# Four residual blocks on one Trainium2 core: the quantized FFN's zero points added by accumulating transfers, and one more down column taken by ScalarE

## The chip, the cores and the metric

One Trainium2 chip (trn2), one core of it. The metric is the device time of one execution in microseconds (us), lower is better. The engines are named PE (TensorE), DVE (VectorE), ACT (ScalarE), POOL (GpSimd) and SP (SyncE, which here only issues transfers).

## The reference

`x` is 8 x 128 x 512 in float32, 1024 tokens of width 512. Four residual blocks follow each other, each behind a layer norm:

```
x = x + xattn0(ln(x), ctx)
x = x + ffn0(ln(x))                 # dense 512x512 plus one of four LoRA ranks, routed per token
x = x + xattn1(ln(x), ctx, mask)    # 32 query heads, 8 key/value heads of 128
x = x + ffn1(ln(x))                 # below
```

The change is about the last block. Its weights are integers 0 to 15 stored as int32, with a zero point and a scale per group of 128 rows and column:

```
dequantize(w, s, z) = (w - repeat(z, 128)) * repeat(s, 128)
gate = silu(x @ dequantize(gate_w, ...))   # 512 x 1792
up   = x @ dequantize(up_w, ...)
ffn1 = (gate * up) @ dequantize(down_w, ...)   # 1792 x 512
```

## The kernel before, in words

The program is written out by hand: one function, one block per engine, and every wait on a semaphore is written at its place. So the order of instructions on an engine is the order of the code, and SP's order is that of the transfers on its queue.

Float32 products are made from a rounded part (hi) and the rest (lo): ACT rounds by a copy into a float32r tile, POOL or DVE subtracts to get the rest, and PE adds two or three products (`three`, `product`).

The stages by time: first attention to about 65 us, keys of the second attention and the dense FFN up to about 150, values, then the attention proper in STEPS = 64 steps (8 key/value groups by 8 token tiles of 128) from about 190 to 660, then the FFN to the end. In an attention step query and probability blocks are transposed by DVE inside 32x32 blocks and turned across blocks through DRAM: SP issues four writes and one read (`bounce_write`, `bounce_read`, tensor `block_bounce`). Within a step POOL scales the probabilities, makes the rms and the rests.

The last stage is cut into UNITS = 14 units of 128 of the 1792 inner columns. A unit's weights are three pieces of 128 x 512 (gate, up, down), loaded as one 128 x 1536 int32 tile. Two halves of `kv` alternate (`unit_raw(par, which)`): weights beside a tile of the zero points, which the load spreads over all 128 rows. POOL subtracts (`sub_gate`, `sub_up`, `sub_down`, L722), ACT rounds the difference into `split` (`gate_ready`, `up_ready`, `down_ready`, L1042). The scales are applied behind the products, since a scale belongs to an output row of the transposed product.

All products of the stage are transposed: 128 rows of columns or hidden units by 1024 tokens in a pair of PSUM banks. There are four such pairs. PE works through 12 items for each unit, four matmuls each:

```
ORDER = (("G", 0), ("E", 2), ("G", 1), ("E", 3), ("G", 2), ("G", 3),
         ("U", 0), ("U", 1), ("U", 2), ("D", 0), ("D", 1), ("U", 3))
```

G and U are the four parts of gate and up of unit i, D the down columns 0 and 1 of unit i-1, E the down columns 2 and 3 of unit i-2. The position of an item (0 to 11) names it. An item's pair is free again only when an engine has taken the item out: DVE takes the positions V_POS, ACT the positions A_POS, and position 11 is summed in its bank and multiplied with the silu of the gate by DVE (L1571), which gives the hidden values of the unit:

```
V_POS, A_POS = (1, 2, 4, 5, 7, 8, SIDE), (0, 3, 6, 9)      # SIDE is position 10
```

A take by DVE scales and adds at once (L1554, into `accT` for down columns). A take by ACT (`take`, L1170) can only scale, so for a down column it writes a temporary, `tmp_a` for column 0 and `tmp_b` for column 3, and POOL adds that to `accT` (`add_down`, L745). ACT rounds the hidden values (`hidden_hi`, L1175), POOL takes the rest (`hidden_lo`, L736), and D of the next unit's round waits for it. Unit 1 has no E items, unit 0 has a code of its own (`first`), and the last unit ends with code of its own (`last_sum`, `last_added`, L1661, L1674).

In a unit POOL's order is: down subtraction of this unit, rest of the hidden values, gate subtraction of the next unit, add of column 3, up subtraction of the next unit, add of column 0. ACT's order is: take of position 0, rounding of hidden values, up weights, take of 3, down weights, scales, take of 6, silu, gate weights of the next unit, take of 9.

SP loads the weights and the zeros of units 0 and 1 while attention runs (`FIRST_UNITS`: at steps 30, 33, 53 and 55, as the key groups there fall free) and each later unit in a loop, once ACT has rounded the up and the down weights of the unit two before it.

## Time and profile before

| what | value |
|---|---|
| median of 3 runs | 833.52 us (832.99 to 834.08) |
| the profiled execution | 834.1 us |
| its span in the profile | 832.3 us |
| busy share PE, DVE, ACT, POOL | 98%, 68%, 64%, 66% |
| granted TensorE clock | full speed throughout |
| HBM | 155 GB/s over the span |

The span is the time from the first to the last instruction that the profile records; the execution's own time is a little longer. Shares are means over stages with different limits, so each stage is read for itself. A row of the view in order of time gives an instruction's start, its duration, engine and line, and in brackets how long its engine stood idle before it and who released it. The durations of two neighbours on one engine overlap a little, so the time that one costs its engine is the distance to the next start.

### The profile page before, as it was taken

How to read it: one execution, taken by the hardware profiler on the slowest of the kernel's cores; microseconds unless marked ns; L12 is line 12 of the kernel's file. 1: busy time of each engine (PE TensorE's matmuls, PEld its weight loads, DVE VectorE, ACT ScalarE, POOL GpSimd, SP SyncE). 2: the span in 40 equal slices, each digit the busy share in tenths (PEclk: the TensorE clock that was granted, in tenths of full speed). 3: DMA queues.
4: the chain of work that ended last, by engine and by line, in shares of the span. 5: the costliest groups of instructions: out<-in, count | busy, mean ns of one | idle time of the engine just before them, and what ended most of it. 6: DMA issues, size and time to landing. Idle time of an engine off the chain costs nothing. (4 is left out here: it accounts for less than half of the span.)

```text
span 832.3 us, 13343 instructions
## 1 busy us (share of the span) xinstructions
PE 816.9 (98%) x3952; PEld 674.3 (81%) x3952; DVE 563.3 (68%) x993; ACT 533.0 (64%) x1773; POOL 549.8 (66%) x555
## 2 busy tenths in 40 slices
PE   8999999999999999999999999999998999999996
PEld 7887888888778888888888888888886777777775
DVE  6416755433666666666666666666657899999997
ACT  4633652245777777777776777777758467677774
POOL 3432642322677777777777777777757268999997
PEclk9999999999999999999999999999999999999999
DMA  9412667105676666666667766666764024443312
GB/s 316 160 37 62 162 166 195 50 1 151 178 203 195 188 188 187 187 182 189 187 187 226 227 191 184 191 191 182 201 193 152 1 76 152 152 152 136 117 52 102
DMA packets 96199, 130.02 MB, mean 156 GB/s; under 512 B 25792, under 2 KB 68672, under 8 KB 96128
## 3 DMA queue, kind: packets, MB, share of 16 engines
q1 hardware_dynamic: 95696, 128.39, 51.5%
q8 instruction: 32, 0.52, 0.3%
q10 hardware_dynamic: 432, 0.79, 0.3%
q14 instruction: 39, 0.32, 0.1%
HBM read 90.08 MB, written 39.06 MB: 155 GB/s over the span
## 5 line engine op out<-in xcount | busy, mean ns | idle before, releaser
L1687 PE MATMUL pair<-split,xnT_hi 128*128 128x512 f32 x288 | 112.6, 391 | 0.4 <-issue 0.3
L1689 PE MATMUL pair<-split,xnT_lo 128*128 128x512 f32 x288 | 112.1, 389 | 0.0
L1688 PE MATMUL pair<-split,xnT_hi 128*128 128x512 f32 x288 | 112.1, 389 | 0.0
L1027 ACT ACTIVATE headT<-land,wqk 128x512 f32<-128x512 f32 x62 | 44.9, 724 | 99.4 <-DMA land<-block_bounce 91.9
L1687 PE MATMUL pair<-split,aoT_hi 128*128 128x512 f32 x244 | 95.9, 393 | 0.0
L1689 PE MATMUL pair<-split,aoT_lo 128*128 128x512 f32 x244 | 95.3, 391 | 0.0
L1688 PE MATMUL pair<-split,aoT_hi 128*128 128x512 f32 x244 | 94.9, 389 | 0.0
L1855 PE MATMUL pair<-xnT_hi,split 128*128 128x512 f32 x224 | 90.7, 405 | 1.8 <-DVE kv L1609 1.0
L1038 ACT ACTIVATE prob<-pair,nmax 128x128 f32<-128x128 f32 x244 | 85.5, 360 | 7.1 <-DVE nmax L1464 6.9
L1856 PE MATMUL pair<-xnT_lo,split 128*128 128x512 f32 x224 | 87.6, 391 | 0.0
L771 POOL TENSOR_TENSOR prob<-prob,rinv 128x512 f32<-128x512 f32 x61 | 63.5, 1041 | 35.7 <-DVE rinv L1435 35.7
L1435 DVE RECIPROCAL rinv<-rsum 128x4 f32<-128x4 f32 x61 | 10.9, 178 | 109.6 <-ACT prob L1038 109.6
L1554 DVE SCALAR_TENSOR_TENSOR kv<-pair,gu_s,kv 128x1024 f32<-128x1024 f32 x65 | 82.3, 1281 | 1.6 <-ACT kv L1170 0.3
L795 POOL TENSOR_TENSOR probT_lo<-land,probT_hi 128x512 fp32r<-128x512 f32 x60 | 77.4, 1290 | 4.4 <-ACT probT_hi L988 1.2
L1458 DVE SCALAR_TENSOR_TENSOR pair<-pair,rms,mask_sb 128x128 f32<-128x128 f32 x248 | 70.0, 351 | 11.5 <-PE pair L1949 11.5
L762 POOL TENSOR_TENSOR split<-raw,split 128x512 fp32r<-128x512 f32 x55 | 70.9, 1289 | 1.6 <-ACT split L970 1.5
L1687 PE MATMUL pair<-split 128*128 128x512 f32 x174 | 70.5, 405 | 1.1 <-DVE split L1294 0.7
L1949 PEld LDWEIGHTS pair<-kv,headT 128*128 128x128 f32 x496 | 64.7, 191 | 5.7 <-ACT headT L1027 0.9
L1003 ACT ACTIVATE pair<-pair 128x128 f32<-128x128 f32 x248 | 68.1, 277 | 0.0
L1689 PE MATMUL pair<-split 128*128 128x512 f32 x174 | 68.1, 391 | 0.0
L1688 PE MATMUL pair<-split 128*128 128x512 f32 x174 | 67.8, 390 | 0.0
L1450 DVE STREAM_TRANSPOSE tb<-pair 128x512 f32<-128x512 f32 x64 | 45.2, 707 | 32.0 <-PE pair L1689 31.7
(202 smaller groups left out, 2161.5 us busy)
## 6 DMA issues: line engine op xcount, KB each, us to landing
block_bounce<-tb SPq DMA_DIRECT2D x244, 128.0 KB, 2.3
land<-block_bounce SPq DMA_DIRECT2D x61, 512.0 KB, 3.6
raw<-in_wqo_dram SPq DMA_DIRECT2D x62, 256.0 KB, 3.1
kv<-in_ffn_w_dram SPq DMA_DIRECT2D x14, 768.0 KB, 4.4
kv<-in_ffn_z_dram SPq DMA_DIRECT2D x14, 768.0 KB, 5.7
kv<-key_bounce SPq DMA_DIRECT2D x32, 128.0 KB, 3.0
key_bounce<-tb SPq DMA_DIRECT2D x44, 64.0 KB, 2.1
resid<-in_x_dram SPq DMA_DIRECT2D x2, 1024.0 KB, 8.4
```

The source lines that it names most:

```text
L762: pool.tensor_tensor(chunk_dst(WGRP + n, 1), raw[:, n % 2, :], as32(chunk_dst(WGRP + n, 0)), ALU.subtract).then_inc(s_lo, 1)
L795: pool.tensor_tensor(by_head(probT_lo[:]), landed(i + PLAG, 1), as32(by_head(probT_hi[:])), ALU.subtract).then_inc(s_ptl, 1)
L1003: done = act.activation(bank[5][:, tile(h)], bank[i % 2][:, tile(h)], ACT.Square, accum_out=ssq[:, i % 2, h:h + 1])
L1038: done = act.activation(prob[:, tile(h)], bank[2 + i % 2][:, tile(h)], ACT.Exp, bias=nmax[:, h:h + 1], accum_out=rsum[:, h:h + 1])
L1458: done = dve.scalar_tensor_tensor(out=cur, in0=cur, scalar=rms[:, i % 4, h:h + 1], in1=mask_sb[:], op0=ALU.mult, op1=ALU.add)
L1554: done = dve.scalar_tensor_tensor(out=cur if in_place else dst, in0=cur, scalar=scale, in1=acc, op0=ALU.mult, op1=ALU.add)
L1687: pe.matmul(dst, l_hi, r_hi, start=first, stop=False)
L1688: pe.matmul(dst, l_hi, r_lo, start=False, stop=False)
L1689: return pe.matmul(dst, l_lo, r_hi, start=False, stop=last)
L1855: pe.matmul(dst, w, r_hi, start=True, stop=False)
L1856: return pe.matmul(dst, w, r_lo, start=False, stop=True)
L1949: done = pe.matmul(bank[2 + i % 2][:, tile(h)], headT[:, tile(h)], cols, start=True, stop=True)
```

## The change

1. In the last stage the third down column (E of column 2, position 1) is taken by ACT instead of DVE in all units from 2 on, ahead of ACT's rounding of the hidden values. It goes into `tmp_c` and POOL adds it (for unit 2 it goes into `accT` directly). DVE's down column 2 in the last unit waits for POOL's last add.
2. The zero points are no longer subtracted by POOL's arithmetic. Early in the kernel they are loaded densely, negated by POOL and stored in DRAM (`negated_zeros`). In the last stage `kv` holds four slots of weights instead of two of weights and two of zeros; SP loads a unit's weights into its slot, and POOL issues a transfer that adds that unit's negated zeros from DRAM, spread over the 128 rows, to the integers in the slot (`zeros_off`). ACT's gate rounding waits for that transfer.
3. For units 0 and 1 this is done in DRAM before attention: SP copies the two units' weights to `first_units` behind the value weights' loads, POOL issues two accumulating transfers onto it. SP then loads the finished units at steps 30 and 36.
4. The loads of units 2 and 3 follow the last bounce, those of later units are issued four units ahead; the loop on SP is written out.

```diff
+        zneg_scr = nc.dram_tensor("negated_zeros", (UNITS, 3 * D), I32, kind="Internal").ap()
+        first_scr = nc.dram_tensor("first_units", (2, P, 3 * D), I32, kind="Internal").ap()
...
-        def unit_raw(par, which):
-            a = (2 * par + which) * UW
+        SLOTS = 4
+        def unit_raw(n):
+            a = n % SLOTS * UW
             return kv[:, a:a + UW]
...
-        FIRST_UNITS = {30: (0, 0), 33: (0, 1), 53: (1, 0), 55: (1, 1)}
+        FIRST_UNITS = {30: 0, 36: 1}
+        READY = 2
...
-        V_POS, A_POS = (1, 2, 4, 5, 7, 8, SIDE), (0, 3, 6, 9)
+        V_POS, A_POS = (2, 4, 5, 7, 8, SIDE), (0, 1, 3, 6, 9)
...
+                    sp.dma_start(zero, zeros_flat(ffn_z)).then_inc(s_zl, 16)
...
+                if m == T + 3:
+                    sp.wait_ge(s_zn, 2)
+                    sp.dma_start(zeros_flat(zneg_scr), zneg).then_inc(s_zs, 16)
...
             weights(WVAL + KT, WGRP)
+            sp.dma_start(first_scr, ffn_w[0:READY]).then_inc(s_fc, 16)
...
-            def load_part(i, par, which):
-                src = (ffn_w[i], ffn_z[bass.ds(i, 1), :].to_broadcast([P, UW]))[which]
-                sp.dma_start(unit_raw(par, which).bitcast(I32), src).then_inc(s_uw[par], 16)
+            def load_unit(n):
+                sp.dma_start(unit_raw(n).bitcast(I32), first_scr[n] if n < READY else ffn_w[n]).then_inc(s_uw[n % SLOTS], 16)
...
+            sp.wait_ge(s_c, BODY * 3)
+            for n in range(READY, SLOTS):
+                load_unit(n)
+            for n in range(SLOTS, UNITS):
+                sp.wait_ge(s_uu, n - SLOTS + 1)
+                sp.wait_ge(s_ud, n - SLOTS + 1)
+                load_unit(n)
...
+                if m == 7:
+                    pool.wait_ge(s_zl, 16)
+                    pool.tensor_tensor(zneg, zero, zero, ALU.subtract).then_inc(s_zn, 1)
+                    pool.wait_ge(s_zn, 1)
+                    pool.tensor_tensor(zneg, zneg, zero, ALU.subtract).then_inc(s_zn, 1)
...
+            pool.wait_ge(s_zs, 16)
+            pool.wait_ge(s_fc, 16)
+            for n in range(READY):
+                pool.dma_start(first_scr[n], zneg_scr[n:n + 1, :].to_broadcast([P, UW]), accum_op=ALU.add)\
+                    .then_inc(s_fz, 16)
             for c in range(WGRP, WGRP + KT):
                 lo(c)
...
+            def zeros_off(n):
+                pool.wait_ge(s_uw[n % SLOTS], 16 * (n // SLOTS + 1))
+                pool.dma_start(unit_raw(n).bitcast(I32), zneg_scr[n:n + 1, :].to_broadcast([P, UW]), accum_op=ALU.add)\
+                    .then_inc(s_uz[n % SLOTS], 16)
...
             def unit(i, p):
-                more = p is not None or i < LAST
-                sub_down(i, p)
                 hidden_lo(i - 1, p)
-                if more:
-                    sub_gate(i + 1, p)
-                if p is not None or i >= 3:
+                if i >= 3:
+                    add_down(i - 2, p, 2)
                     add_down(i - 2, p, 3)
-                if more:
-                    sub_up(i + 1, p)
+                if i + 2 < UNITS:
+                    zeros_off(i + 2)
                 if p is not None or i >= 2:
                     add_down(i - 1, p, 0)
...
             for j in range(-LEAD, DRAIN + 1):
                 step(j, None)
-                if j == STEPS - 10:
-                    sub_gate(0, None)
-                if j == STEPS - 9:
-                    sub_up(0, None)
-                if j == STEPS - 8:
-                    sub_down(0, None)
...
+                if e == 0:
+                    zeros_off(READY)
...
             def gate_ready(i, p):
-                act.wait_ge(s_sg, unit_at(p, i) + 1)
+                if i < READY:
+                    act.wait_ge(s_uw[i], 16)
+                else:
+                    act.wait_ge(s_uz[i % SLOTS], 16 * (i // SLOTS + (i % SLOTS >= READY)))
...
                 take(i, p, 0, gated(par), gu_s[:, par, 0:1])
+                if not skipped(i, p, 1):
+                    if i == 2:
+                        act.wait_ge(s_ds, 1)
+                    elif i >= 4:
+                        act.wait_ge(s_p2, n - 3)
+                    take(i, p, 1, accT[:, 2, :] if i == 2 else tmp_c, down_s[:, par, 2:3])
                 hidden_hi(i - 1, p)
...
                 dve.wait_ge(s_gs, n + 1)
-                if not skipped(i, p, 1):
-                    take_down(i, p, 1, 2, p is None and i == 2)
```

The order of POOL's instructions in a middle unit of the last stage before, with `split<-tb` the rest of the hidden values, `kv<-kv 128x512` the integer subtractions and `kv<-kv 128x1024` the adds of columns 3 and 0:

```order
L736 TENSOR_TENSOR split<-tb,split 128x1024
L722 TENSOR_TENSOR kv<-kv 128x512
L745 TENSOR_TENSOR kv<-kv 128x1024
L722 TENSOR_TENSOR kv<-kv 128x512
L745 TENSOR_TENSOR kv<-kv 128x1024
L722 TENSOR_TENSOR kv<-kv 128x512
L736 TENSOR_TENSOR split<-tb,split 128x1024
```

And the same place now:

```order
L757 TENSOR_TENSOR split<-tb,split 128x1024
L763 TENSOR_TENSOR kv<-kv 128x1024 x2
L751 DMA kv<-negated_zeros 128x1536
L763 TENSOR_TENSOR kv<-kv 128x1024
L757 TENSOR_TENSOR split<-tb,split 128x1024
```

The three subtractions are gone, the adds of columns 2 and 3 stand together, and the transfer is issued between them and the add of column 0.

ACT in a middle unit before, from the take of position 0 on (`kv<-pair,gu_s` takes of gate and up, `kv<-pair,down_s` takes of down columns, `split<-tb` the rounding of hidden values, `split<-kv` weights; the number behind `pair` is the PSUM pair):

```order
L1170 ACTIVATE kv<-pair1,gu_s 128x1024
L1175 ACTIVATE split<-tb 128x1024
L1042 ACTIVATE split<-kv 128x512
L1170 ACTIVATE kv<-pair1,down_s 128x1024
L1042 ACTIVATE split<-kv 128x512
L1152 ACTIVATE down_s<-gds 128x4
```

And now, from the take of position 1 on:

```order
L1182 ACTIVATE kv<-pair0,down_s 128x1024
L1187 ACTIVATE split<-tb 128x1024
L1053 ACTIVATE split<-kv 128x512
L1182 ACTIVATE kv<-pair1,down_s 128x1024
L1053 ACTIVATE split<-kv 128x512
L1164 ACTIVATE down_s<-gds 128x4
```

The new take of pair 0 stands directly ahead of the rounding; the rest is as before.

SP at the end of attention before (`block_bounce` and `land` are the bounce, one write of four pieces and one read a step):

```order
L608 DMA block_bounce<-tb 32x4x256 x4
L639 DMA kv<-in_ffn_z_dram 128x1536
L619 DMA land<-block_bounce 128x1024
L608 DMA block_bounce<-tb 32x4x256 x4
L619 DMA land<-block_bounce 128x1024
```

And now:

```order
L629 DMA block_bounce<-tb 32x4x256 x4
L640 DMA land<-block_bounce 128x1024
L629 DMA block_bounce<-tb 32x4x256 x4
L640 DMA land<-block_bounce 128x1024
L659 DMA kv<-in_ffn_w_dram 128x1536 x12
```

The load of unit 1's zeros is gone from ahead of a read, and all twelve later loads follow the last read.

## Rows read from the trace of the kernel before

**Rows 1.** Stretches, last stage: us, busy (instructions) PE, PEld, DVE, ACT, POOL, clock, DMA.
```profile
730.00:760.00 30.00, 29.99 (x128) 23.45 (x128) 29.50 (x25) 21.43 (x31) 29.18 (x17) 1.00 0.43 158
```
**Rows 2.** DVE in order of time, one unit: start us, us, what, [idle before].
```profile
704.16 1.23 DVE L1571 TENSOR_TENSOR tb<-pair,kv 128x1024 f32<-128x1024 f32 x1
705.30 1.28 DVE L1554 SCALAR_TENSOR_TENSOR kv<-pair,down_s,kv 128x1024 f32<-128x1024 f32 x1
706.50 6.43 DVE L1554 SCALAR_TENSOR_TENSOR kv<-pair,gu_s,kv 128x1024 f32<-128x1024 f32 x5
...
715.48 1.23 DVE L1571 TENSOR_TENSOR tb<-pair,kv 128x1024 f32<-128x1024 f32 x1
```
**Rows 3.** PE in order of time, unit 1 and a wait in unit 4.
```profile
676.86 0.39 PE L1855 MATMUL pair<-split 128*128 128x512 f32 x1
...
684.80 0.39 PE L1856 MATMUL pair<-xnT_lo,split 128*128 128x512 f32 x1
...
707.83 0.19 PEld L1855 LDWEIGHTS pair<-xnT_hi,split 128*128 128x128 f32 x1 [0.43 <-DVE kv L1554]
```
**Rows 4.** Waits, 640 to 820 us: us in total, times, longest.
```profile
PEld pair L1855 <- DVE kv L1554: 8.5, 24, 0.5
```
**Rows 5.** POOL in order of time, one unit.
```profile
797.07 2.42 POOL L736 TENSOR_TENSOR split<-tb,split 128x1024 fp32r<-128x1024 f32 x1 [0.41 <-ACT split L1175]
799.44 1.30 POOL L722 TENSOR_TENSOR kv<-kv 128x512 int32<-128x512 int32 x1
...
808.38 2.41 POOL L736 TENSOR_TENSOR split<-tb,split 128x1024 fp32r<-128x1024 f32 x1 [0.40 <-ACT split L1175]
```
**Rows 6.** ACT in order of time, one unit.
```profile
793.77 1.12 ACT L1170 ACTIVATE kv<-pair,gu_s 128x1024 f32<-128x1024 f32 x1 [1.54 <-PE pair L1856]
795.93 1.06 ACT L1175 ACTIVATE split<-tb 128x1024 fp32r<-128x1024 f32 x1 [1.04 <-DVE tb L1571]
...
799.56 1.12 ACT L1170 ACTIVATE kv<-pair,gu_s 128x1024 f32<-128x1024 f32 x1 [0.34 <-PE pair L1856]
...
801.92 0.61 ACT L1042 ACTIVATE split<-kv 128x512 fp32r<-128x512 int32 x1
```
**Rows 7.** Transfers: KB each, us to landing; two issues by SP in order of time.
```profile
kv<-in_ffn_w_dram SPq DMA_DIRECT2D x14, 768.0 KB, 4.4
kv<-in_ffn_z_dram SPq DMA_DIRECT2D x14, 768.0 KB, 5.7
...
94.35 1.25 SPq L525 DMA_DIRECT2D raw<-in_wffn_dram  x1
...
697.43 0.33 SPq L639 DMA_DIRECT2D kv<-in_ffn_w_dram  x1
697.95 0.52 SPq L639 DMA_DIRECT2D kv<-in_ffn_z_dram  x1
```
**Rows 8.** End of attention, in order of time by engine; first the bounce read's landing.
```profile
land<-block_bounce SPq DMA_DIRECT2D x61, 512.0 KB, 3.6
...
615.30 0.43 SPq L639 DMA_DIRECT2D kv<-in_ffn_z_dram  x1
617.79 0.34 SPq L619 DMA_DIRECT2D land<-block_bounce  x1
...
622.30 0.72 ACT L1027 ACTIVATE headT<-land,wqk 128x512 f32<-128x512 f32 x1 [3.68 <-DMA land<-block_bounce]
...
625.07 1.27 POOL L722 TENSOR_TENSOR kv<-kv 128x512 int32<-128x512 int32 x1
...
627.00 0.47 PE L1687 MATMUL pair<-probT_hi,vcur_hi 128*128 128x512 f32 x1 [0.89 <-DVE aoT_lo L1421]
...
633.35 0.66 PE L1995 MATMUL pair<-ident,prob 128*128 128x128 f32 x4 [1.07 <-POOL prob L809]
```
**Rows 9.** POOL in order of time, ahead of attention.
```profile
175.73 2.71 POOL L673 TENSOR_TENSOR split<-raw,split 128x512 fp32r<-128x512 f32 x2 [17.43 <-ACT split L871]
```
**Rows 10.** POOL in order of time, last unit.
```profile
814.87 2.40 POOL L745 TENSOR_TENSOR kv<-kv 128x1024 f32<-128x1024 f32 x1 [1.72 <-ACT kv L1170]
```

More of the change, by code:

```diff
@@ L130, in cross_attention_ffn, with zeros_flat @@
         xnT32 = kv[:, 3 * QUART:4 * QUART].rearrange("p (m n) -> p m n", m=KT)
+        zneg_scr = nc.dram_tensor("negated_zeros", (UNITS, 3 * D), I32, kind="Internal").ap()
+        first_scr = nc.dram_tensor("first_units", (2, P, 3 * D), I32, kind="Internal").ap()
+        zero, zneg = (kv[:, 3 * QUART - (k + 1) * UNITS * 3 * D // P:3 * QUART - k * UNITS * 3 * D // P].bitcast(I32)
+                      for k in range(2))
+        def zeros_flat(ap):
+            return ap.rearrange("u n -> (u n)").rearrange("(p c) -> p c", p=P)
         o = 2 * QUART
@@ L391, in cross_attention_ffn @@
         s_plo = sem("late_probs_lo")
-        s_uw = [sem("unit_loaded0"), sem("unit_loaded1")]
-        s_sg = sem("unit_gate_zero_sub")
-        s_su = sem("unit_up_zero_sub")
-        s_sd = sem("unit_down_zero_sub")
+        s_zl = sem("zeros_loaded")
+        s_zn = sem("zeros_negated")
+        s_zs = sem("negated_zeros_stored")
+        s_fc = sem("first_units_copied")
+        s_fz = sem("first_units_zeros_added")
+        s_uw = [sem(f"unit_loaded{i}") for i in range(SLOTS)]
+        s_uz = [sem(f"unit_zeros_added{i}") for i in range(SLOTS)]
         s_ug = sem("unit_gate_ready")
@@ L411, in cross_attention_ffn @@
         s_pb = sem("down_added_from_b")
+        s_p2 = sem("down_added_from_c")
         s_p1 = sem("last_down_one_added")
@@ L485, in item @@
             return 6 * KT + 2 + ITEMS * (n - 2) + pos + 1
-        V_POS, A_POS = (1, 2, 4, 5, 7, 8, SIDE), (0, 3, 6, 9)
+        V_POS, A_POS = (2, 4, 5, 7, 8, SIDE), (0, 1, 3, 6, 9)
         def by_vector(n, pos):
             if isinstance(n, int) and n == 1:
-                return 6 + sum(k != 1 for k in V_POS if k <= pos)
+                return 6 + sum(k <= pos for k in V_POS)
             return 12 + len(V_POS) * (n - 2) + V_POS.index(pos) + 1
@@ L497, in by_scalar @@
             if isinstance(n, int) and n == 1:
-                return 8 + sum(k != 3 for k in A_POS if k <= pos)
+                return 8 + sum(k not in (1, 3) for k in A_POS if k <= pos)
             return 11 + len(A_POS) * (n - 2) + A_POS.index(pos) + 1
@@ L643, in _ @@
                 if j in FIRST_UNITS:
-                    par, which = FIRST_UNITS[j]
-                    sp.wait_ge(s_c, BODY * -(-(par + 1) * 2 * UW // (2 * TOK)))
-                    load_part(par, par, which)
-            with sp.Fori(0, UNITS // 2 - 1) as p:
-                for u in range(2):
-                    sp.wait_ge(s_uu, 2 * p + u + 1)
-                    sp.wait_ge(s_ud, 2 * p + u + 1)
-                    for which in range(2):
-                        load_part(2 * p + u + 2, u, which)
+                    n = FIRST_UNITS[j]
+                    sp.wait_ge(s_fz, 16 * READY)
+                    sp.wait_ge(s_c, BODY * -(-(n + 1) * UW // (2 * TOK)))
+                    load_unit(n)
[5 more added lines that the diff above has]
+                sp.wait_ge(s_ud, n - SLOTS + 1)
+                load_unit(n)
             for t in range(T):
@@ L947, in copy_values @@
             def copy_values(m):
+                if m == 0:
+                    act.wait_ge(s_zs, 16)
                 act.wait_ge(s_v, m + 1)
@@ L1041, in ready @@
             def ready(i, p, cols, part, done):
-                act.activation(unit_w(i % 2, part), unit_raw(i % 2, 1)[:, cols].bitcast(I32), ACT.Copy).then_inc(done, 1)
+                act.activation(unit_w(i % 2, part), unit_raw(i)[:, cols].bitcast(I32), ACT.Copy).then_inc(done, 1)
             def gate_ready(i, p):
-                act.wait_ge(s_sg, unit_at(p, i) + 1)
+                if i < READY:
+                    act.wait_ge(s_uw[i], 16)
+                else:
+                    act.wait_ge(s_uz[i % SLOTS], 16 * (i // SLOTS + (i % SLOTS >= READY)))
                 if i < 2 and p is None:
@@ L1190, in unit @@
                 if p is not None or i >= 2:
-                    act.wait_ge(s_tv, by_vector(n, 1))
+                    act.wait_ge(s_tv, by_vector(n - 1, SIDE))
                 down_ready(i, p)
@@ L1235, in _ @@
             take(LAST, None, 9, tmp_a, down_s[:, 1 - LAST % 2, 0:1])
+            act.wait_ge(s_p2, LAST - 2)
             take(LAST, None, SUM, tmp_c, down_s[:, 1 - LAST % 2, 1:2])
```

24 lines of the change are left out of this document (3 added, 21 removed).

## The prediction

> **What bounds the kernel now.** I read the table of stretches first, then the instructions in order of time on each engine for one unit of the last stage (the fourth residual block, an FFN cut into 14 units), then the waits, the transfers, and the two ends of the stage. "Unit" below is one of those 14, G, U, D, E the products of ORDER.
>
> In the middle of the stage PE and DVE are both marked busy for nearly all of 30 us, at the full granted clock, POOL for 29.18, ACT for 21.43 [rows 1]. DVE paces it: from one product with the silu (L1571) to the next are 715.48 - 704.16 = 11.32 us, and DVE has no idle time in it: 1.14, a down take of 1.20, five takes of 6.43, a down take, the sum [rows 2]. PE needs less: 35 matmuls apart are 684.80 - 676.86 = 7.94 us, so 0.2269 each and 48 x 0.2269 = 10.89 us a unit; it loses the other 0.43 in two short waits for a DVE take, one of them shown [rows 3]. The waits of the stage list 24 of them, two in each of units 2 to 13 [rows 4]. POOL is close behind: the rest of the hidden values costs it 799.44 - 797.07 = 2.37, and there are two adds of the same length and three integer subtractions of 1.30 in a unit; before that rest it waits only 0.40 for ACT [rows 5]. ACT waits 1.54 us before its first take and 1.04 before the rounding of the hidden values [rows 6].
>
> **Edit 1, the third column's take from DVE to ACT.** Removed from DVE: one take of 706.50 - 705.30 = 1.20 us in each of units 2 to 13. DVE then needs 11.32 - 1.20 = 10.12 us. PE's 10.89 is the next bound, worth 11.32 - 10.89 = 0.43 us a unit, 12 x 0.43 = **5.2 us**.
>
> Does another loop stand in the way? Hidden product, ACT's rounding, ACT's items up to the take of U0, DVE's takes of U1, U2, D1, the sum, the product again. ACT: 799.56 - 795.93 = 3.63, of which 0.34 is waiting for PE, so 3.29; the take 1.12; two DVE takes 2.57; then 715.48 - 712.93 = 2.55; product 1.23; handovers 0.1 [rows 2, 6]. That is 10.86 us, beside PE's 10.89. So nothing beyond 5.2 is to be had here, and a delay inside this loop shows at once. The new ACT take is ahead of the rounding, outside it as long as it fits. The first take starts at 793.77 and lasts 1.12, the rounding starts at 795.93: 1.04 us for a take of 1.12. Bounds: nothing, or all of it pushed into the loop (13 us over the stage); I take nothing, since the gap is missed by 0.08 only and the loop has 0.03 in hand.
>
> **Edit 2, zero points by accumulation.** POOL loses three subtractions (3.9 us a unit) and gets one add (2.37) for the new take's temporary and one transfer to issue. POOL's unit is 4 x 2.37 = 9.48 us plus g, what issuing costs POOL itself. The trace has no transfer issued by POOL. Bounds: SP issues such a load in 0.33 us, a whole POOL tile operation is 2.40 [rows 7, 10]. I take g = 1.25, the longest single issue in the trace [rows 7], because POOL must prepare 128 rows with an addition, more than SP's median. POOL's unit is then 10.73, under 10.89: no cost. POOL reaches PE's pace at g = 1.41 and the old pace at g = 1.84.
> The Trainium skill ("DMA: Bandwidth & Descriptors", section Latency and other measured facts) gives about 1 us to the first byte for GpSimd's transfers against 0.6 from SP and ACT; no row here shows one. An estimate by it, with g at 1 us, puts POOL's unit at 10.5 us and leaves the sum as it is.
>
> The transfer itself takes L. Loads of 768 KB land in 4.4 us (weights) and 5.7 (zeros, right behind them) [rows 7]. An addition needs its destination read as well, so twice the reading: the pair took 0.52 + 5.7 = 6.2 us. L lies between 4.4 and 4.4 + 5.7 = 10.1 (both reads one after the other); I take 6.2, the pair side by side. Room for it: POOL starts the hidden rest at 797.07, two adds bring it to 797.07 + 3 x 2.37 = 804.18, there it issues; ACT's take 0 of that unit was at 793.77, so 10.4 us after it. Behind the landing come ACT's gate rounding (0.6) and the product and handover (1.2) before take 0 two units later. The chain is 10.4 + g + L + 1.8 in two units: no cost while g + L < 2 x 10.89 - 12.2 = 9.6. With 7.45 it is covered, and its cover is 2 us; if that is gone ACT stands before the gate rounding, with the take of D0 and POOL's add behind it. Loads no longer share a moment with the zeros, since four slots let SP load four units ahead.
>
> **Edit 3, two units in DRAM.** SP's copy (1.5 MB, one issue) comes behind the last value weights; POOL's two transfers come ahead of rounding rests that begin at 175.73 after 17.43 us idle [rows 9]. Two new POOL operations on 168 columns in the key stage and one small store and load on SP lie under PE's products. I cost all of it at nothing. If the additions in DRAM lasted into the attention stage, they would slow its bounces; unit 0 is not read for another 200 us.
>
> **Edit 4, what leaves the end of attention.** There SP issued unit 1's zeros at 615.30, ahead of the bounce read of 617.79, whose landing let ACT go on at 622.30: 4.5 us instead of the median 3.6. That chain ends in PE's wait of 0.89 at 627.00. POOL's subtraction of 625.07 to 626.30 stands ahead of a probability product and of the next wait, 1.07 at 633.35 [rows 8]. Both go. I take 0.9 for the first and 0.4 for the second, since PE itself arrives earlier there: **1.3 us**; bounds 0 and 0.89 + 1.07 = 2.0. Units 2 and 3 are now loaded right behind the last bounce read instead of being ahead of anything: nothing.
> **The end.** POOL's extra add in the last unit falls into its 1.72 us wait, 0.65 too long; the two halves it adds last start about 0.3 later, and DVE and the transposes wait for them [rows 10]: **+0.2 us**, between 0 and 0.65.
>
> **Sum:** -5.2 - 1.3 + 0.2 = -6.3 us. The profiled execution took 834.1 us around a span of 832.3; that is 0.6 above the median of the runs, 833.52. On the median: **827.2 us**. About 0.2% (1.7 us) is what a measurement can tell from no change.
>
> **Rivals.**
> (a) *POOL becomes the bound, partly.* g between 1.4 and 1.85 gives units of 10.9 to 11.3. At 1.65 it is 11.13: nine units (3 to 11) save 0.19 and three 0.43, 3.0 in all; 833.5 - 3.0 - 1.1 = 829.4 us. For: POOL was busy 29.18 of 30. Chance 0.10.
> (b) *POOL becomes the bound, worse than before.* g = 2.4: 11.88 a unit, 9 x (11.88 - 11.32) = +5.0, less 1.3 in the other three and 1.1 at the ends: 836.1 us. It decides from g = 1.84. DVE is never idle, so anything by which it kept POOL from writing the transfer's descriptors would show in g; against it, POOL's own tile operations beside that full DVE take an even 2.40 to 2.42 [rows 5]. The Trainium skill ("SBUF — State Buffer", section Who interferes with whom) says that VectorE's two-port modes lock GpSimd out of a shared port pair, its descriptor writes included. Chance 0.10.
> (c) *The accumulating transfer is too slow.* It decides from g + L = 9.6 and is slower than before from 2 x 11.32 - 12.2 = 10.4. At the upper bound, 1.25 + 10.1 = 11.35, a unit is 11.8: ten units (those behind transfers that POOL issues late) lose 0.46, less 2.0 gained elsewhere: 836.1 us. At L = 12 it is 12.7 a unit: +14 - 2 = 845.5 us. For: no row shows how fast the transfer engines add. Against: 2 us of cover at the value taken. Chance 0.18.
> (d) *The change does not do what it says:* the third take pushes into the loop by what DVE was relieved of, 0.4 us a unit. ACT's gap is short by 0.08 only, but the loop has no slack. 12 x 0.43 goes, the ends stay: 832.4 us. Chance 0.06.
> The forecast case keeps 0.56.
>
> **From cases to numbers.** The forecast's own range is 825.0 to 829.0. Faster by over 0.2% is the forecast and nearly all of (a): 0.65. Within 0.2% is (d) and a sliver of (a): 0.07. Slower is (b) and (c): 0.28. The range runs from 825.0 to 838: above it lies most of (c) with L over 10 and the worst of (b), about 0.15, below it 0.04.
>
> **What would show it.** Right: 10.9 us from one L1590 product to the next (line of the new file), DVE with an idle of 0.5 to 1 us a unit waiting for PE or ACT, PE without waits for DVE takes, POOL with four 2.4 us operations a unit and a gap of about 1.2, ACT's gate rounding without a wait for a transfer, the wait at 627 gone. Wrong: ACT waiting for the kv<-negated_zeros transfer before the gate rounding (rival c); POOL without idle and PE or ACT waiting for the hidden rest (a, b); PE waiting for ACT's take of E3 or DVE's of U1 at 11.3 a unit (d); PE waits between 187 and 600 us would mean that the DRAM additions are not hidden.

## The result and the profile after

| | before | changed |
|---|---|---|
| median of the runs, us | 833.35 (832.99 to 834.08, 4 runs) | 828.54 (827.71 to 828.77, 4 runs) |
| ratio to before | | 0.9934, 95% interval 0.9922 to 0.9945 |
| profiled execution, us | 834.1, span 832.3 | 828.77, span 827.0 |
| busy, 730 to 760 us: PE, DVE, ACT, POOL | [rows 1] | 30.00, 27.78, 24.44, 28.31 |

The changed kernel is faster by 0.66% (0.55 to 0.78%): 4.8 us between the medians, 5.3 between the two spans. The prediction was 827.2 us, within 825 to 838. Five more runs of the same kernel, beside other runs of before, gave 828.06 and the ratio 0.9934 again.

The middle of the FFN stage, in the table of stretches of the changed kernel (us, then busy time and instructions of PE, PEld, DVE, ACT and POOL, the granted clock, the DMA share), answers to [rows 1]:

```profile
730.00:760.00 30.00, 30.00 (x134) 24.84 (x133) 27.78 (x23) 24.44 (x32) 28.31 (x15) 1.00 0.62 151
```

DVE has got room, ACT has taken the work, PE completes more matmuls in the same 30 us (134 in place of 128). One unit of DVE in order of time [rows 2]:

```profile
702.38 1.22 DVE L1590 TENSOR_TENSOR tb<-pair,kv 128x1024 f32<-128x1024 f32 x1
703.53 1.27 DVE L1573 SCALAR_TENSOR_TENSOR kv<-pair,gu_s,kv 128x1024 f32<-128x1024 f32 x1
705.21 2.60 DVE L1573 SCALAR_TENSOR_TENSOR kv<-pair,gu_s,kv 128x1024 f32<-128x1024 f32 x2 [0.41 <-PE pair L1874]
708.11 2.60 DVE L1573 SCALAR_TENSOR_TENSOR kv<-pair,gu_s,kv 128x1024 f32<-128x1024 f32 x2 [0.29 <-ACT kv L1182]
...
713.27 1.23 DVE L1590 TENSOR_TENSOR tb<-pair,kv 128x1024 f32<-128x1024 f32 x1
```

From product to product are 713.27 - 702.38 = 10.89 us, and DVE now waits twice, for PE and for ACT. Of PE's 24 waits for a DVE take [rows 4], 8.5 us in all, one of 0.5 us is left between 640 and 820 us. ACT in the same unit [rows 6]:

```profile
701.57 1.12 ACT L1182 ACTIVATE kv<-pair,gu_s 128x1024 f32<-128x1024 f32 x1 [1.58 <-PE pair L1874]
702.59 1.11 ACT L1182 ACTIVATE kv<-pair,down_s 128x1024 f32<-128x1024 f32 x1
703.64 1.06 ACT L1187 ACTIVATE split<-tb 128x1024 fp32r<-128x1024 f32 x1
...
708.91 0.62 ACT L1053 ACTIVATE split<-kv 128x512 fp32r<-128x512 int32 x1
709.75 1.12 ACT L1182 ACTIVATE kv<-pair,down_s 128x1024 f32<-128x1024 f32 x1 [0.22 <-PE pair L1874]
```

The new take (down_s, 702.59) fills the wait of 1.04 us that stood ahead of the rounding (it costs ACT 703.64 - 702.59 = 1.05), and the gate rounding of 708.91 waits for no transfer. POOL [rows 5]:

```profile
704.78 2.42 POOL L757 TENSOR_TENSOR split<-tb,split 128x1024 fp32r<-128x1024 f32 x1 [0.49 <-ACT split L1187]
707.14 4.79 POOL L763 TENSOR_TENSOR kv<-kv 128x1024 f32<-128x1024 f32 x2
711.85 0.88 POOL L751 DMA_DIRECT2D kv<-negated_zeros  x1
712.46 2.70 POOL L763 TENSOR_TENSOR kv<-kv 128x1024 f32<-128x1024 f32 x1
715.67 2.42 POOL L757 TENSOR_TENSOR split<-tb,split 128x1024 fp32r<-128x1024 f32 x1 [0.51 <-ACT split L1187]
```

Issuing the transfer costs POOL 0.9 us: the next add starts 0.61 behind it and takes 2.70 in place of 2.40. POOL still idles 0.5 a unit. The transfers of the stage (KB each, us from issue to landing) answer to [rows 7]:

```profile
kv<-negated_zeros POOLq DMA_DIRECT2D x12, 768.0 KB, 6.7
kv<-in_ffn_w_dram SPq DMA_DIRECT2D x9, 768.0 KB, 4.4
```

The same view gives for each queue its packets, the MB and the share of the time of the 16 transfer engines (640 to 820 us; q0 is POOL's, q1 SP's):

```profile
q0 software_dynamic: 1728, 9.44, 28.5%
q1 hardware_dynamic: 1378, 7.48, 12.5%
```

So a MB of the accumulating transfers takes the transfer engines 1.8 times as long as a MB on SP's queue (28.5 / 9.44 against 12.5 / 7.48). It goes with this that from 730 to 760 us the DMA share rose from 0.43 to 0.62 although fewer GB/s are moved (151 against 158).

**Where the 5.3 us of the spans came from**, by marks that both traces have: the row maxima of the 64 attention steps on DVE (TENSOR_REDUCE into `nmax`, one a step, called steps 0 to 63 below; "step 42 takes" means the time from maximum 41 to maximum 42), the products, and the end. These numbers are not those of SP's loop (`FIRST_UNITS`): a load that SP issues at its step 36 goes out between maxima 40 and 41, and what it costs shows at maximum 42, six on.

| piece | before | changed | difference |
|---|---|---|---|
| start to step 0 | 202.41 | 203.13 | +0.72 |
| steps 0 to 35 | 241.79 | 241.46 | -0.33 |
| steps 35 to 58 | 161.94 | 162.79 | +0.85 |
| steps 58 to 63 | 32.95 | 30.78 | -2.17 |
| step 63 to the first product | 28.43 | 28.43 | 0 |
| first product to the last sum of the last unit | 147.26 | 142.09 | -5.17 |
| last sum to the end of the span | 17.52 | 18.32 | +0.80 |

The start varies from one execution to the next: over the fourteen traces of the study step 0 stands at 202.26 to 203.13, in no order by kernel, and steps 0 to 35 take 241.3 to 243.3. The four other differences were tested.

### The profile page after: what moved, and what is told of

Read it like the earlier page. It is cut to its first block, busy times and chain, and to the rows that moved or that the text cites. A ratio compares the mean times of both kernels' runs of the same rounds, so it can differ in the third digit from the quotient of the medians.

```text
span 827.0 us, 13239 instructions
## 1 busy us (share of the span) xinstructions
PE 813.4 (98%) x3952; PEld 677.3 (82%) x3952; DVE 550.9 (67%) x981; ACT 545.8 (66%) x1785; POOL 536.2 (65%) x540
## 4 chain that ended last, share of the span: by engine, by line
PE 87%; DMA 4%; POOL 2%; ACT 2%; DVE 2%; issue 1%; SPq 1%; POOLq 0%; ACTq 0%; DVEq 0%
PE pair L1705 20%; PE pair L1707 20%; PE pair L1706 20%; PE pair L1873 8%; PE pair L1874 8%; PE pair L1967 6%; DMA land<-block_bounce 2%; PE pair L1727 2%; DMA block_bounce<-tb 1%; PE pair L1769 1%; PE pair L1820 1%; POOL kv L763 1%; PE pair L1797 1%; SPq L629 1%; ACT prob L1049 1%
## 5 line engine op out<-in xcount | busy, mean ns | idle before, releaser
L1873 PE MATMUL pair<-xnT_hi,split 128*128 128x512 f32 x224 | 88.1, 393 | 1.7 <-DVE kv L1626 1.0
L763 POOL TENSOR_TENSOR kv<-kv 128x1024 f32<-128x1024 f32 x34 | 83.9, 2484 | 2.9 <-ACT kv L1182 2.9
```

The lines of the kernel that those rows point to most:

```text
L763: pool.tensor_tensor(accT[:, c, :], accT[:, c, :], tmp, ALU.add).then_inc(done, 1)
L1873: pe.matmul(dst, w, r_hi, start=True, stop=False)
```

## Experiments

Ratios are to the kernel before, measured beside each, with their 95% interval. The first four ran beside 15 runs of before (833.48), the next four beside 9 (833.81), the last four beside 17 (833.64).

### The take without the accumulating transfers

Kernel before, third column's take to ACT, its add on POOL, subtractions kept:

```diff
-        V_POS, A_POS = (1, 2, 4, 5, 7, 8, SIDE), (0, 3, 6, 9)
+        V_POS, A_POS = (2, 4, 5, 7, 8, SIDE), (0, 1, 3, 6, 9)
...
                 if i >= 3:
+                    add_down(i - 2, p, 2)
                     add_down(i - 2, p, 3)
```

> The kernel before with the third column's take moved to ACT (and POOL's add for it), and the zero points still subtracted by POOL. Theory A, the one of the prediction (POOL's three subtractions had to go first): POOL's unit becomes 4 adds or rests of 2.37 and 3 subtractions of 1.30, 13.4 us against 11.3; about ten units cost 2.1 each, so some 21 us slower than before, near 854, with POOL never idle in the stage. Rival B (POOL's durations are stretched by DVE's full load, and shrink once DVE idles): little slower or even faster, 828 to 836.

Measured: 853.04 us, ratio 1.023 (1.0215 to 1.0246). The last products stand 13.2 us apart (782.04 to 821.58 for three units), and POOL is busy 40.00 of the 40 us from 780 to 820. POOL in order of time:

```profile
787.88 2.45 POOL L737 TENSOR_TENSOR split<-tb,split 128x1024 fp32r<-128x1024 f32 x1
790.19 1.39 POOL L723 TENSOR_TENSOR kv<-kv 128x512 int32<-128x512 int32 x1
791.44 4.88 POOL L743 TENSOR_TENSOR kv<-kv 128x1024 f32<-128x1024 f32 x2
```

Theory A holds: without the transfers the same relief of DVE costs 20 us. Rival B falls: DVE now idles more, and POOL's adds got longer, not shorter (median 2.50 us against 2.42 before). TensorE's granted clock fell to 0.50, the lower of its two levels, at 738.2 to 741.2 us and at 765.6 to 768.6, each behind a wait of PE of 2.0 us for POOL (a third such wait, at 724.59, was followed by no fall). That is not where the 20 us come from: from 780 to 820 us the clock is 1.00 and the unit is 13.2 us all the same, and the units around the two falls average 13.2 as well.

### The transfers without the take

Changed kernel, position 1 back in V_POS with DVE's take, no add_down(i - 2, p, 2).

> The changed kernel with the third column's take back on DVE and without POOL's add for it; zero points by accumulating transfers stay. Theory A: DVE paces the FFN stage again at 11.3 us a unit, only the end of attention gains; 831 to 832, PE waiting twice a unit for DVE. Rival B (the gain in the FFN stage comes from the subtractions or the transfers of zeros being gone, not from DVE's take): 828 to 829, a unit near 10.9.

Measured: 833.33 us (831.84 to 834.24, 11 runs), ratio 1.0002 (0.9993 to 1.0011). In the trace the products are 11.31 us apart again, POOL is busy only 20.82 of 30 us, DVE 29.54:

```profile
730.00:760.00 30.00, 30.00 (x131) 23.77 (x130) 29.54 (x25) 20.76 (x28) 20.82 (x11) 1.00 0.63 156
```

So with the transfers in place the whole gain of the FFN stage comes from moving DVE's take, as A says, and none from the smaller number of POOL operations; B falls. Together with the run before it: either edit alone gains nothing there. But A's 831 to 832 was missed. Steps 58 to 63 take 30.78 here too, so the 2.17 us is there; steps 35 to 58 lose 0.50. That leaves 1.7 to be seen, and the median shows 0.15, give or take 0.75. The traced execution, 831.84, is the fastest of the eleven, so its terms say little about where the others spend their 1.5 us more. The loss in steps 35 to 58 is taken up below.

### ACT's take behind its rounding

```diff
                 take(i, p, 0, gated(par), gu_s[:, par, 0:1])
+                hidden_hi(i - 1, p)
                 if not skipped(i, p, 1):
...
                     take(i, p, 1, accT[:, 2, :] if i == 2 else tmp_c, down_s[:, par, 2:3])
-                hidden_hi(i - 1, p)
```

> The changed kernel with ACT's take of the third column put behind its rounding of the hidden values instead of ahead of it. Theory A (the loop product, rounding, ACT's items, take of U0, DVE, product was estimated at 10.86 us, beside PE's 10.88, so nothing may be put into it): the take of 1.05 us lengthens the loop to 11.9, 10 to 12 units, so 10 to 12 us slower than the changed kernel, near 840. Rival B (the loop has more room than the sum of its terms says, since its waits overlap): 828 to 832.

Measured: 839.85 us, ratio 1.0075 (1.0059 to 1.009). The products stand 11.84 us apart (695.97, 707.80, 719.64, ...), 0.96 more than in the changed kernel. ACT there:

```profile
742.51 1.12 ACT L1182 ACTIVATE kv<-pair,gu_s 128x1024 f32<-128x1024 f32 x1 [1.58 <-PE pair L1874]
744.58 1.06 ACT L1187 ACTIVATE split<-tb 128x1024 fp32r<-128x1024 f32 x1 [0.95 <-DVE tb L1590]
745.54 1.10 ACT L1182 ACTIVATE kv<-pair,down_s 128x1024 f32<-128x1024 f32 x1
```

Now ACT idles 0.95 ahead of the rounding and does the take after it. The loop of 10.86 us is real and has 0.1 us of room at most: 1.05 put into it costs 0.96 in every unit.

### The zeros issued 2.4 us later

```diff
+                if p is not None or i >= 2:
+                    add_down(i - 1, p, 0)
                 if i + 2 < UNITS:
                     zeros_off(i + 2)
-                if p is not None or i >= 2:
-                    add_down(i - 1, p, 0)
```

> The changed kernel with POOL's transfer of a unit's zeros issued behind its last add of the unit instead of ahead of it, 2.4 us later. Theory A (issue plus landing of 6.7 us leaves 1.2 us ahead of ACT's gate rounding and about 1.2 behind it, where ACT waits for PE anyway): ACT now waits about 1.2 us for the transfer in most units, the product of the next unit's gate is just in time; 828.5 to 831. Rival B (every microsecond by which the zeros come after ACT wants them is paid): 1.2 us a unit over ten units, near 840. Rival C (the landing shrinks or grows with what else the queues do, so no wait appears): 828.5 and no wait of ACT for the transfer.

Measured: 829.6 us (828.2 to 830.85), ratio 0.9956 (0.994 to 0.9971). Products are 10.88 us apart as before the edit. The waits from 680 to 800 us (in total, times, longest) have a new line that the changed kernel lacks:

```profile
ACT split L1053 <- DMA kv<-negated_zeros: 7.6, 9, 1.2
```

and ACT's later waits for PE shrink by it, from 21.4 us (23 waits) to 13.4 (13). A holds in the trace: the zeros come up to 1.2 us late and no unit gets longer. How much more delay the stage would bear this run does not show. The median lies 1.1 us above that of the changed kernel (828.54); with four runs each, 828.2 to 830.85 against 827.71 to 828.77, and no unit longer in the trace, where that comes from stays open.

### The end: POOL's add in two halves

```diff
-            pool.tensor_tensor(accT[:, 3, :], accT[:, 3, :], tmp_b, ALU.add).then_inc(s_pb, 1)
+            for h in range(2):
+                pool.tensor_tensor(accT[:, 3, half(h)], accT[:, 3, half(h)], tmp_b[:, half(h)], ALU.add).then_inc(s_pb, 1)
```

(and the two later waits on s_pb one higher). The lines of the changed kernel that it aims at, POOL, DVE and PE in order of time, answer to [rows 10] and what follows it:

```profile
814.52 2.39 POOL L864 TENSOR_TENSOR kv<-kv 128x1024 f32<-128x1024 f32 x1
...
817.04 2.07 DVE L1692 SCALAR_TENSOR_TENSOR kv<-pair,down_s,kv 128x512 f32<-128x512 f32 x3 [0.65 <-POOL kv L864]
...
817.84 3.71 PE L2123 MATMUL pair<-ident,kv 128*128 128x128 f32 x32 [1.08 <-DVE kv L1692]
```

> The changed kernel with POOL's last whole add (column 3, 2.37 us) cut into two halves, so that DVE can go on after the first. Theory A (the end of the changed kernel costs 0.8 us because POOL's add for the third column pushed that add back, and DVE and the transposes wait for it): DVE's wait of 0.65 us for POOL goes, and the last product to the end of the program is 0.4 to 0.7 us shorter than in the changed kernel; 827.9 to 828.2. Rival B (the transposes wait for the last half adds anyway, which come no earlier): no gain, 828.5.

Measured: 828.19 us, ratio 0.9928 (0.9915 to 0.9942). DVE's wait is gone, and PE has another:

```profile
816.74 1.97 PE L2124 MATMUL pair<-ident,kv 128*128 128x128 f32 x16 [0.32 <-DVE kv L1693]
819.33 1.94 PE L2124 MATMUL pair<-ident,kv 128*128 128x128 f32 x16 [0.63 <-POOL kv L858]
```

From the last sum to the end of the span it is 18.1 us in place of 18.3. Mostly B: the second half of the transposes waits for POOL's last adds, which come no earlier.

### Unit 1's load back at step 53

What cost 0.85 us in steps 35 to 58 of the changed kernel? Steps 36 to 41 of it take 0.07 too long together; the rest lies in steps 42 to 45, behind the load that SP issues at its step 36. SP's issues, ACT's wait and the maxima from step 41 on, in order of time:

```profile
480.30 0.46 SPq L613 DMA_DIRECT2D raw<-in_wqo_dram  x1
480.85 0.39 SPq L659 DMA_DIRECT2D kv<-first_units  x1
482.72 0.32 SPq L640 DMA_DIRECT2D land<-block_bounce  x1
...
486.85 0.69 DVE L1483 TENSOR_REDUCE nmax<-pair 128x4 f32<-128x512 f32 x1
488.00 0.72 ACT L1038 ACTIVATE headT<-land,wqk 128x512 f32<-128x512 f32 x1 [3.31 <-DMA land<-block_bounce]
...
494.56 0.69 DVE L1483 TENSOR_REDUCE nmax<-pair 128x4 f32<-128x512 f32 x1
500.97 0.69 DVE L1483 TENSOR_REDUCE nmax<-pair 128x4 f32<-128x512 f32 x1
509.57 0.69 DVE L1483 TENSOR_REDUCE nmax<-pair 128x4 f32<-128x512 f32 x1
515.87 0.69 DVE L1483 TENSOR_REDUCE nmax<-pair 128x4 f32<-128x512 f32 x1
```

The steps take 7.71, 6.41, 8.60 and 6.30 us where 7.06 is the rule: 29.02 for 28.24. The load of unit 1 stands in the queue between a chunk of weights (`raw<-in_wqo_dram`) and the bounce read.

```diff
-        FIRST_UNITS = {30: 0, 36: 1}
+        FIRST_UNITS = {30: 0, 53: 1}
```

> The changed kernel with the load of unit 1 issued at step 53 of the attention stage, where no chunk of weights is loaded any more, as it was before, instead of at step 36. Theory A (the attention stage gives back what its end gained: at step 36 the 768 KB stand between a chunk of weights and the bounce read, whose landing comes late for ACT, and PE loses 0.5 to 1 us there in every profile of the changed kernel's family, and nothing in those of the kernel before): steps 42 to 45 of the maxima run at 7.03 to 7.06 us each, and the median falls by 0.8 to 1.5 us, to 827.0 to 827.7. Rival B (the loss in the middle of the attention stage is chance, another load would show it as well): 828.5, with a step of 8 us somewhere behind 53.

Measured: 828.34 us, ratio 0.9934 (0.992 to 0.9947). The maxima of the same steps:

```profile
487.12 0.69 DVE L1483 TENSOR_REDUCE nmax<-pair 128x4 f32<-128x512 f32 x1
494.18 0.69 DVE L1483 TENSOR_REDUCE nmax<-pair 128x4 f32<-128x512 f32 x1
501.24 0.69 DVE L1483 TENSOR_REDUCE nmax<-pair 128x4 f32<-128x512 f32 x1
508.30 0.69 DVE L1483 TENSOR_REDUCE nmax<-pair 128x4 f32<-128x512 f32 x1
515.36 0.69 DVE L1483 TENSOR_REDUCE nmax<-pair 128x4 f32<-128x512 f32 x1
```

7.06 each. In the traces A's loss is there with unit 1's load at SP's step 36 (0.5 to 1.0 us over steps 35 to 58 in five traces, 3.1 in a sixth, of which 2.0 at maximum 36, behind unit 0's load) and it is 0.0 to 0.1 in the five traces without a load between SP's steps 34 and 52. The median did not follow: 828.34 beside 828.54 and 828.06 of the changed kernel is within what five runs can tell. The loss is shown, its worth on the median is not.

### What gained at the end of attention

Kernel before, unit 1's weights and zeros at steps 48 and 50 instead of 53 and 55; in the second run POOL's subtractions for unit 0 at STEPS - 20, - 18, - 16 instead of - 10, - 9, - 8 as well.

```diff
-        FIRST_UNITS = {30: (0, 0), 33: (0, 1), 53: (1, 0), 55: (1, 1)}
+        FIRST_UNITS = {30: (0, 0), 33: (0, 1), 48: (1, 0), 50: (1, 1)}
```

> The kernel before with unit 1's weights and zeros loaded at steps 48 and 50 of the attention stage instead of 53 and 55, POOL's subtractions left where they are. Read from the last six maxima of the attention stage alone (steps 58 to 63, 32.95 us before, 30.78 after the change). Theory A (the zeros' load at step 55 delays the bounce read and costs the first wait; the subtractions cost the second): about half of the 2.17 us goes, 31.5 to 32.3. Rival B (the load does it all): 30.8. Rival C (POOL's subtractions do it all): 32.9. At steps 48 and 50 the loads may cost something of their own, seen earlier in the stage.

> As the run before it, and POOL's three subtractions for unit 0 eight to ten steps earlier, out of the end of the attention stage. Theory A: both waits are gone and steps 58 to 63 take 30.8 us, as in the changed kernel. Rival B (the load does it all): 30.8 here and 30.8 in the run before it. Rival D (neither, it is the two subtractions of unit 1 that stay at the end): over 32.

One run each: 834.95 and 833.24 us. The maxima of steps 58 and 63 in the first, load alone:

```profile
609.19 0.69 DVE L1464 TENSOR_REDUCE nmax<-pair 128x4 f32<-128x512 f32 x1
...
639.97 0.69 DVE L1504 TENSOR_REDUCE nmax<-pair 128x4 f32<-128x512 f32 x1
```

639.97 - 609.19 = 30.78, as in the changed kernel, and 30.78 again with the subtractions moved. Rival B: with the two loads gone from the stage's end all of the 2.17 us is gained, and the subtractions that stay there cost nothing. The opposite case, the loads left and the subtractions moved, was not run, so whether the subtractions add to what the loads cost is not shown. The price turns up where the loads went: steps 53 to 58 take 37.49 us (second run 35.65) where before they took 35.19.

### The changed kernel again, and two combinations

> The changed kernel once more, as the base of the three runs beside it: 828.0 to 828.8 on the median. Its trace, a second one, tells which losses come back: if the loss of 0.5 to 1.1 us in the maxima of steps 42 to 45 is the place of unit 1's load, it is there again; if it is chance, it may be gone.

Measured: 828.06 us (827.86 to 828.72), ratio 0.9934 (0.9921 to 0.9946). Its trace has the loss again (step 42 takes 8.40 us), and the same two waits at the end (0.64 and 1.08 us).

Both combinations add column 3 in halves and take its last piece by DVE, with ACT's take and POOL's add of that piece dropped and the waits behind them moved; they differ in FIRST_UNITS, {30: 0, 53: 1} and {53: 0, 55: 1}:

```diff
-            for e, (h, c) in enumerate(((1, 0), (1, 3))):
-                last_added(e, h, c)
+            last_added(0, 1, 0)
...
-            for h, c in ((0, 0), (0, 1), (0, 2), (0, 3), (1, 1), (1, 2)):
+            for h, c in ((0, 0), (0, 1), (0, 2), (0, 3), (1, 1), (1, 2), (1, 3)):
```

> Unit 1's load at step 53, POOL's add of column 3 in halves, and the last piece of column 3 (second half) taken by DVE itself from PSUM, 0.68 us, in place of a take by ACT and an add by POOL of 1.26. Theory A (in the run with halves alone DVE's wait went, and PE's second transposes waited for POOL's last add in its place, so POOL's chain of adds itself must be shorter): DVE's wait and PE's wait for POOL both go, the last product to the end is 0.5 to 0.8 us shorter than in the changed kernel, and with the load 0.6 to 1.5 us go in all: 827.0 to 827.9. Rival B (DVE's seventh take delays the transposes by what POOL's add did): as the changed kernel's end, 828.0 to 828.5.

> As the run beside it, but unit 0's load at step 53 and unit 1's at step 55, so that no load of 768 KB stands beside the chunks of weights. Theory A (each such load in the middle costs the attention stage something in many executions, also the one at step 30: the profile with the rounding first lost 2 us there): steps 36 and 37 of the maxima run at 7.03 too, the median is 0 to 1.5 us below the run beside it. Rival B (without the zeros' load in front of it, step 55 is still too late: the end of the stage has less room than its middle): a maximum of 8 us or more among steps 59 to 61, and up to 2 us slower than the run beside it.

Measured: 827.84 us, ratio 0.9929 (0.9916 to 0.9941), and 828.69 us, ratio 0.9938 (0.9925 to 0.9952). In both traces DVE's and PE's waits for POOL are gone. The first, from the seven takes on:

```profile
814.24 4.70 DVE L1692 SCALAR_TENSOR_TENSOR kv<-pair,down_s,kv 128x512 f32<-128x512 f32 x7 [0.20 <-DVE kv L1679]
...
817.03 3.94 PE L2123 MATMUL pair<-ident,kv 128*128 128x128 f32 x32 [0.35 <-DVE kv L1692]
...
818.83 3.73 POOL L869 TENSOR_TENSOR resid<-resid,kv 128x512 f32<-128x512 f32 x3 [0.61 <-ACT kv L1272]
```

POOL's last work ends 13.95 us after the last sum, against 14.69 in the changed kernel: the 0.7 us is gained. But from there to the end of the span are 4.3 us, against 3.6. The issues from 818 us on (KB each, us to landing) differ too:

```profile
out_dram<-resid ACTq DMA_DIRECT2D x3, 256.0 KB, 3.7
```

In the changed kernel this line reads 3.1, and in the run with halves alone 2.9. The eight outputs are now issued within 3.5 us (819.57 to 823.03) in place of 4.0 (819.73 to 823.73) and land later; the end is their landing, and the gain is gone. That the closer issues are what slows the landing fits these three traces but was not tested by itself. With both loads late, steps 36 and 37 run at 7.03, but step 61 takes 8.15 and steps 58 to 63 take 31.87: a load at step 55 costs 1.09 us even without zeros in front of it. Neither combination can be told from the changed kernel; 827.84 is the lowest median of the study.

### Without the work in DRAM

Units 0 and 1 loaded from the input, their zeros added in SBUF by POOL's transfers inside its attention loop:

```diff
-            for n in range(READY):
-                pool.dma_start(first_scr[n], zneg_scr[n:n + 1, :].to_broadcast([P, UW]), accum_op=ALU.add)\
-                    .then_inc(s_fz, 16)
...
+                if j in (40, 46):
+                    if j == 40:
+                        pool.wait_ge(s_zs, 16)
+                    zeros_off((j - 40) // 6)
```

> The changed kernel without the copy of units 0 and 1 in DRAM and the two additions there: their weights are loaded from the input at the same steps 30 and 36, and POOL issues the two additions in SBUF at steps 40 and 46 of its attention stage. Theory A (the additions in DRAM lie under PE's products and cost nothing, and so do two issues of 0.9 us inside the attention stage): as the changed kernel, 828.0 to 828.8. Rival B (the DRAM work, 11 MB on POOL's queue ahead of the stage, or reading those units from the scratch tensor is what keeps the end of attention's gain out of the median): 1 to 2 us faster than the changed kernel. Rival C (issues and additions inside the attention stage disturb its bounces): slower by 0.5 to 3 us, with losses in the maxima near steps 40 to 48.

Measured: 832.96 us (831.2 to 839.14, 12 runs), ratio 1.0003 (0.9985 to 1.0022); 4.9 us slower than the changed kernel beside it. The profiled execution took 837.38; it is one of the three slowest of the twelve (837.38, 838.96, 839.14), and these three alone have a mean granted clock of 0.995, the other nine 0.997 to 1.000. POOL issues at 510.90, SP the bounce read at 511.48, and ACT and PE then:

```profile
520.34 0.72 ACT L1035 ACTIVATE headT<-land,wqk 128x512 f32<-128x512 f32 x1 [6.84 <-DMA land<-block_bounce]
...
524.70 0.76 PE L1699 MATMUL pair<-probT_hi,vcur_hi 128*128 128x512 f32 x1 [2.42 <-DVE aoT_lo L1434]
```

The bounce read lands 8.8 us after its issue (the median of the stretch from 495 to 540 us is 3.8), and step 46 takes 11.08 us. Behind PE's wait of 2.42 us the granted clock is at 0.50, the lower of its two levels, for 6.6 us, in the table of stretches:

```profile
523.80:530.40 6.60, 5.70 (x14) 4.47 (x15) 3.93 (x10) 4.44 (x20) 5.80 (x7) 0.50 0.58 161
```

Step 47 falls into it and takes 9.03 us, where the step behind a late read takes 6.3 elsewhere. So a part of this trace's loss, by an estimate 9.03 - 6.3 = 2.7 us, is the clock's and only indirectly the transfer's, and by their mean clock most of the twelve runs do not have it. The second addition, at a clock of 1.00, costs 2.7 us: steps 52 and 53 take 10.48 and 6.27. Rival C, stronger than it was put: the 4.9 us of the median hardly hang on the three executions at 0.995 (832.89 without them). Rival B falls, and its 11 MB are POOL's queue over the whole program; ahead of attention come only two of its fourteen transfers. In the DRAM version POOL's two issues lie in its idle time:

```profile
158.99 1.90 POOL L744 DMA_DIRECT2D first_units<-negated_zeros  x2
176.45 2.72 POOL L695 TENSOR_TENSOR split<-raw,split 128x512 fp32r<-128x512 f32 x2 [15.57 <-ACT split L880]
```

## Why the prediction was right, and where it was not

**Edit 1, right.** Forecast -5.2, measured -5.17, by the forecast's own mechanism: DVE's 11.32 gave way to PE's 10.89. The take fitted into ACT's gap (no wait ahead of the rounding at 703.64), so rival (d) did not come; that the loop has nothing in hand is shown by the rounding put first, 0.96 us a unit.

**Edit 2, right, with both unknowns inside their bounds.** g was taken as 1.25 and is 0.9; L was taken as 6.2 and is 6.7, and the two errors offset each other. Their sum of 7.6 us against the estimate's 7.45 leaves a cover of 2 us. It was understated: the later issue took 2.4 us (9.48 us behind the start of the hidden rest in place of 7.07) and lengthened no unit. Rivals (a), (b) and (c) did not come. The source of 1.25 was misread: it is not the longest single issue of the trace, which has one of 1.80 us (and one of 2.26 for a bounce write):

```profile
465.79 1.80 SPq L592 DMA_DIRECT2D raw<-in_wqo_dram  x1
```

With g = 1.80 the sum would have put POOL's unit at 11.28 and hardly any gain, so the choice of 1.25 was in part luck. The mechanism feared in (b) left no sign: with DVE busy 27.78 of 30 us the twelve issues took 0.84 to 0.97 us. The Trainium skill's "SBUF — State Buffer", section Who interferes with whom, names that lockout; no run here shows it acting on these issues. From 680 to 800 us DVE ran only TENSOR_TENSOR and SCALAR_TENSOR_TENSOR, each with an operand in PSUM, so what another form would do to the issues is untested. That POOL would have been the bound without the transfers is shown: 13.2 us a unit where 4 x 2.37 + 3 x 1.30 = 13.4 was worked out.

**Edit 3, right in itself.** The DRAM additions cost nothing that a trace shows; what the prediction did not say is what they are for. The same additions during attention cost 4.9 us. Its sign of being wrong, PE waits between 187 and 600 us, did appear (steps 42 to 45), but not from the additions: they go with unit 1's load to step 53 while the additions stay.

**Edit 4, wrong twice.** "I take 0.9 for the first and 0.4 for the second": the gain at the end of attention is 2.17 us, above the stated bound of 2.0, and it goes with the loads of unit 1 at steps 53 and 55. The subtraction that I held responsible for 0.4 of the 1.3 costs nothing once the loads are elsewhere. And the step "Units 2 and 3 are now loaded right behind the last bounce read ...: nothing" passed over that unit 1's load moved too, from step 53 to 36, into the steps that still load chunks; it loses 0.5 to 1.0 us there. A moved load was counted where it left and not where it arrived.

**The end, mis-sized.** "+0.2 us, between 0 and 0.65" is +0.80. POOL's chain in the last unit is later by the 0.65 that its extra add exceeds its old wait and by another 0.4, since its hidden rest starts later against the last sum (802.72 to 808.68 = 5.96 us ahead, before 808.38 to 814.78 = 6.40). DVE had 0.4 us of room before it needed that add; it waits for the other 0.65, and the transposes behind it.

**Sum.** Measured terms: -5.17 - 2.17 + 0.85 + 0.80 = -5.7, beside the ratio's -5.5; the forecast of -6.3 left out a loss of 0.85, took the gain at the end of attention 0.9 too small and the loss at the end 0.6 too small. These three errors partly cancel, so that the forecast median came within 1.3 us of the measured one is in part luck; the 5.2 us of the take are not. What stays open: with the transfers alone the median showed 0.15 us where the traces' terms sum to 1.7. Only one execution of each set of runs has a trace, and the middle of the attention stage differs most between executions (step 36 lost 2 us in one of them); whether the others lose more there was not seen.

## What to carry to other kernels

To relieve the busiest engine, first make room on the one that takes the work: the same take cost 20 us without the transfers and gained 5 with them. When a transfer moves, price it at its new place in the queue too: in a stage where the DMA engines are busy 0.68 of the time (400 to 610 us), the same load of 768 KB ahead of a bounce read cost 0.5 to 1.0 us at SP's step 36, 1.1 at step 55 and nothing at step 53. At a tail, follow the chain past the wait that you remove: here it went from DVE to POOL to the landing of the outputs, and each fix gained less than its wait.

## What the runs showed of the hardware

- An accumulating transfer of 768 KB into SBUF lands 6.7 us after its issue in the FFN stage (6.1 to 9.5), a plain load of the same size 4.4. Issued by POOL it costs that engine 0.9 us: 0.6 to the start of the next operation, and 0.3 by which that one is longer. Per MB it takes the transfer engines 1.8 times as long as what goes over SP's queue (28.5% for 9.44 MB, 12.5% for 7.48 MB).
- The same transfer amid bounces took 9.6 us, and the 512 KB bounce read issued 0.6 us behind it landed after 8.8 us instead of 3.8. So a transfer on POOL's queue delays one on SP's; where the two meet the runs do not show.
- POOL's integer subtraction of 128x512 took 1.27 to 1.33 us in the kernel before, and up to 1.46 (median 1.33) in the kernel where POOL never idles in the FFN stage; its adds there took 2.50 at the median and up to 2.57, in place of 2.42 and 2.44. What slows them was not tested.
- In the trace with the additions during attention the granted clock was 0.50 from 523.8 to 530.4 us, behind a wait of TensorE of 2.42 us; the matmuls of 128x512 there follow each other every 0.43 us (525.26 to 525.69) in place of 0.23. The late transfer was followed by two losses, the wait and the clock behind it.
